# Paired product layout, router weights on GpSimd, reordered last chunk and tail in an attention and mixture-of-experts kernel

## The chip, the cores and the metric

One core of a Trainium2 chip runs the whole program. The metric is the device time of one execution in microseconds (us), lower is better. TensorE is called PE, VectorE DVE, ScalarE ACT, GpSimd POOL and SyncE SP. SP issues the plain transfers, POOL issues the gathers and scatters.

## The reference

The model is one gated convolution over a context of shape (8, 256, 512) and one feed-forward layer with 16 experts and a shared expert, both added to `x`. Cut to what matters:

```python
# attention-like mixer: 32 heads of 8 channels, sequence length 512
kv  = einsum('bhil,bhjl->bijhl', k, v)            # k = v = ctx: 36 distinct pairs of channels
y   = causal_convolution(kv, ssm_kernel) + kv * D # one Toeplitz matrix of taps per head
out = einsum('bijhl,bhil->bjhl', y, q)            # q = layernorm(x): 64 products, summed by eights
x   = x + out
# feed-forward
h      = layernorm(x)                             # 2048 tokens of 512
scores = softmax(h @ gate_w.T)                    # 16 experts, top 4, weights normalised
slots  = first 256 tokens of each expert, in order
y      = sum over experts of w * ((silu(xg @ w_gate) * (xg @ w_up)) @ w_down)   # inner width 352
shared = (silu(h @ sw_gate) * (h @ sw_up)) @ sw_down                            # inner width 704
x      = x + y + shared
```

## The kernel before

Every engine has its own program, written out by hand, and semaphores order them. Nothing is planned by a scheduler: what stands first in an engine's program runs first, and a wait holds everything behind it on that engine.

**Precision.** Each fp32 operand of a large product is split in a high part (rounded by ACT) and a low part (the rest, subtracted by POOL or DVE), and three products high*high, high*low, low*high are added (`PASSES`). So each piece of weights or data passes ACT and then DVE or POOL before PE may use it.

**Mixer.** There are 8 groups (`NG`) of 4 heads (`GH`). For head `n`, POOL makes the 36 channel pairs `kv` (`pairs`), ACT and POOL split them, PE multiplies with the Toeplitz blocks into the PSUM tile `yb` (`convolve`, 30 matmuls), DVE multiplies `yb` with the queries into `prod` (`multiply`, 15 instructions on 2048 elements, by halves of 30 instructions for the first four heads) and sums eights of them into `oT` (`add_up`). PE waits with head `n + 1` for the products of head `n` (`d_mul`), since `yb` holds one head.

**Shared expert.** Group `g - 1` is normalised, transposed and passed through `gate_up` (six parts, 24 matmuls each) while group `g` is convolved, and `down(g - 2)` makes its output: two tiles of 17 matmuls each, of which the first two are for the 64 inner columns that are left over from 704 (`REST`). The second of these two has 64 rows, all others have 128.

**Router.** DVE turns the logits into scores, finds the top 4, and computes the weights (`weights`), ranks and slots in two rounds: round 0 for the first 12 tiles of tokens, round 1 for the last 4. `rt_c` and `rt_mm` are the hand-over to three small matmuls and back. `one_hot(e)`, `slots(e)` and `decode(e)` give the token numbers `slot_rows` of expert `e`.

**Experts.** `gather(e)` on POOL fetches 256 rows into `xg`, PE transposes them (`rows_t`), ACT and DVE split them (`round_rows`, `low_rows`), PE runs three `expert_gu` and one `expert_down`, ACT weighs the result (`weigh`) and POOL adds it to the output (`scatter`). SP loads the raw weights `raw_w[k]` (1.4 MB) and `raw_d[k]` of the next experts into two slots, ACT and DVE split them into `ew` and `ed` (`split_w` and `low_w`, four parts each). From expert 1 on, a unit holds: two `expert_gu`, `slots(e + 2)`, `rows_t(e + 1)`, `expert_down(e - 1)`, the third `expert_gu`.

In this order PE leaves the mixer: `mixed_out(7)`, `down(6)`, `normalised(7)`, `gate_up(7, 0)`, router, `gate_up` 1 and 2, the three small matmuls, `gate_up` 3 to 5, `slots(0)`, `down(7)` tile 0, `slots(1)`, tile 1, `rows_t(0)`, `expert_gu(0, 0)`.

## Time and profile before

| | before |
|---|---|
| median of 3 runs | 664.18 us (661.24 to 664.54) |
| the profiled execution, its own time | 665.34 us |
| its span, first to last instruction | 663.5 us |
| PE busy | 609.0 us, 92% of the span |
| DVE busy | 506.9 us, 76% |
| POOL busy | 344.7 us, 52% |
| ACT busy | 283.6 us, 43% |
| mean granted TensorE clock | 0.973 of full speed |

The profiled execution's own time is 1.8 us above its span, and 1.2 us above the median of the runs. Busy times are sums over a program with three stages (mixer with shared expert to about 370 us, router and last chunk to about 440 us, experts after that), so they say only that PE is the fullest engine. What an edit is worth is read from the stage in which it lies.

### The profile page before, as it was taken

The page shows a single profiled execution, that of the slowest core. Times are in us where ns is not written, and L with a number is a line of the kernel's source. Part 1 is how long each engine was busy: PE and PEld are TensorE (multiplying, and loading weights), DVE is VectorE, ACT ScalarE, POOL GpSimd, SP SyncE. Part 2 cuts the span into 40 slices and gives each one's busy share as a digit, 9 for nine tenths or more (in the row PEclk, how much of TensorE's full clock was granted, in tenths as well). Part 3 has the DMA queues.
Part 4 walks back from the last instruction along what each step waited for, and adds up shares of the span by engine and source line. Part 5 has one row for each costly group of instructions (what it writes and reads, how often), then busy time and mean ns, then how long its engine had stood idle before and what let it go on. Part 6 is the DMA issues. An engine that isn't in the chain of part 4 may idle for free.

```text
span 663.5 us, 13617 instructions
## 1 busy us (share of the span) xinstructions
PE 609.0 (92%) x4487; PEld 568.0 (86%) x4487; DVE 506.9 (76%) x1248; ACT 283.6 (43%) x503; POOL 344.7 (52%) x467
## 2 busy tenths in 40 slices
PE   2867999999999999999999779889999999999982
PEld 2866997999989989989999578789999999999981
DVE  5897978959778778588698958698887878878630
ACT  3433542433423424234241233356656656656530
POOL 5796787856666676668551124216334443334321
PEclk9978999999999999999999989899999999999997
DMA  6664603424225124041130144567888878888442
GB/s 156 201 154 156 191 33 97 126 64 134 59 64 158 63 79 142 32 124 34 63 96 1 48 146 143 172 183 220 250 245 240 226 200 239 240 239 234 95 62 32
DMA packets 50386, 90.31 MB, mean 136 GB/s; under 512 B 3920, under 2 KB 20304, under 8 KB 50336
## 3 DMA queue, kind: packets, MB, share of 16 engines
q1 hardware_dynamic: 43168, 72.89, 35.7%
q0 software_dynamic: 7168, 16.78, 12.1%
q8 instruction: 28, 0.46, 0.3%
q14 instruction: 22, 0.18, 0.1%
HBM read 72.71 MB, written 16.94 MB: 135 GB/s over the span
## 4 chain that ended last, share of the span: by engine, by line
PE 74%; DVE 9%; issue 8%; POOL 4%; DMA 2%; ACT 1%; DVEq 0%; SPq 0%; POOLq 0%; ACTq 0%
PE gu L524 15%; PE yb L461 15%; PE gu L653 13%; PE mb L668 9%; PE gu L549 8%; PE yb L653 6%; PE mb L441 3%; DVE prod L1171 2%; PE yb L441 2%; DVE prod L1174 2%; POOL midl L1009 1%; PE gu L542 1%; DMA sw_raw<-in_L_ffn_sw_up_dram 1%; PE yb L627 1%; DVE oT L1190 1%
## 5 line engine op out<-in xcount | busy, mean ns | idle before, releaser
L461 PE MATMUL yb<-kvh,toep 128*128 128x288 f32 x640 | 140.6, 306 | 10.1 <-DVE prod L1174 8.8
L524 PE MATMUL gu<-xT,sw 128*128 128x256 f32 (+2 forms) x1152 | 144.4, 284 | 3.8 <-issue 3.8
L524 PEld LDWEIGHTS gu<-xT,sw 128*128 128x128 f32 (+2 forms) x1152 | 140.3, 184 | 4.3 <-issue 4.0
L1171 DVE TENSOR_TENSOR prod<-yb,qT 128x96 f32<-128x96 f32 (+11 forms) x288 | 112.5, 418 | 40.3 <-PE yb L461 39.2
L461 PEld LDWEIGHTS yb<-kvh,toep 128*128 128x128 f32 x640 | 109.8, 197 | 12.1 <-issue 9.2
L1001 POOL TENSOR_TENSOR kvl<-kv,kvh 128x1152 fp32r<-128x1152 f32 x31 | 83.4, 2691 | 59.7 <-ACT kvh L750 59.5
L993 POOL TENSOR_TENSOR kv<-kT 128x256 f32 (+3 forms) x248 | 113.3, 498 | 0.0
L461 PE MATMUL yb<-kvl,toep 128*128 128x288 f32 x320 | 97.4, 304 | 0.0
L1174 DVE TENSOR_TENSOR prod<-yb,qT 128x96 f32<-128x96 f32 (+10 forms) x252 | 93.4, 389 | 0.0
L750 ACT ACTIVATE kvh<-kv 128x1152 fp32r<-128x1152 f32 x32 | 37.4, 1168 | 91.4 <-POOL kv L993 48.5
L1190 DVE TENSOR_REDUCE oT<-prod 128x256 f32<-128x2048 f32 x32 | 72.7, 2272 | 0.1
L668 PE MATMUL mb<-ed,midh 128*128 128x512 f32 (+1 forms) x192 | 62.5, 407 | 1.9 <-ACT midh L897 1.9
L1009 POOL TENSOR_TENSOR midl<-mid,midh 128x256 fp32r<-128x256 f32 x40 | 33.1, 835 | 58.7 <-ACT midh L766 48.7
L461 PEld LDWEIGHTS yb<-kvl,toep 128*128 128x128 f32 x320 | 63.1, 197 | 0.0
L1448 DVE TENSOR_TENSOR ew<-raw_w,ew 128x704 fp32r<-128x704 f32 x64 | 55.5, 890 | 0.3 <-ACT ew L862 0.3
L549 PE MATMUL gu<-sd,midh 128*128 128x512 f32 x160 | 51.3, 402 | 0.4 <-POOL midl L1009 0.4
L653 PE MATMUL gu<-xT,ew 128*128 128x256 f32 x384 | 48.4, 287 | 1.8 <-DVE xT L1456 1.8
L653 PEld LDWEIGHTS gu<-xT,ew 128*128 128x128 f32 x384 | 47.6, 195 | 2.0 <-issue 2.0
L1075 POOL MEMSET carrier<- 128x1 f32 x16 | 1.6, 99 | 89.5 <-DVE slot_rows L1442 89.5
L653 PE MATMUL gu<-xgT,ew 128*128 128x256 f32 x384 | 47.2, 282 | 0.6 <-DVE ew L1448 0.6
L653 PEld LDWEIGHTS gu<-xgT,ew 128*128 128x128 f32 x384 | 46.4, 190 | 0.8 <-issue 0.8
L862 ACT ACTIVATE ew<-raw_w 128x704 fp32r<-128x704 f32 x64 | 45.4, 778 | 3.1 <-DMA raw_w<-in_L_ffn_w_up_dram 3.1
(168 smaller groups left out, 1009.5 us busy)
## 6 DMA issues: line engine op xcount, KB each, us to landing
toep<-toeplitz_taps SPq DMA_DIRECT2D x32, 512.0 KB, 3.7
raw_w<-in_L_ffn_w_gate_dram SPq DMA_DIRECT2D x16, 704.0 KB
raw_w<-in_L_ffn_w_up_dram SPq DMA_DIRECT2D x16, 704.0 KB
raw_d<-in_L_ffn_w_down_dram SPq DMA_DIRECT2D x16, 512.0 KB, 4.3
c_t<-in_ctx_dram SPq DMA_DIRECT2D x16, 256.0 KB, 4.7
x_t<-in_x_dram SPq DMA_DIRECT2D x16, 256.0 KB, 4.8
normalised_tokens<-xn SPq DMA_DIRECT2D x16, 256.0 KB, 2.9
out_dram<-yo SPq DMA_DIRECT2D x16, 256.0 KB, 2.9
```

The costliest lines, as they stand in the source:

```text
L461: last = pe.matmul(yb[:, lb, 0:PW], toep[s][:, a, d:d + P], rhs[:, s, m, :], start=(i == 0), stop=(i == len(steps) - 1))
L524: last = pe.matmul(gu[0:m, i % 2, u * GT:(u + 1) * GT], sw[:, c, a, col:col + m], xT[:, c, b, :], start=(c == 0 and (a, b) == PASSES[0]), ...
L549: last = pe.matmul(gu[:, t, :], (midh, midl)[a][:, j, cols], sd[:, j, b, :], start=False, stop=(j == SJ - 2 and (a, b) == PASSES[-1]))
L653: last = pe.matmul(egu[j][0:m, u * CAP:(u + 1) * CAP], ew[k][:, c, a, col:col + m], xgT[k][:, c, b, :], start=(c == 0 and (a, b) == PASSES ...
L668: last = pe.matmul(mb[:, h, :], lhs[0:EK[j], EJ * k + j, h * P:(h + 1) * P], ed[k][0:EK[j], j, b, :], start=(j == 0 and (a, b) == PASSES[0 ...
L862: act.activation(ew[k][:, c, 0, :], raw_w[k][:, c, :], ACT.Copy).then_inc(ew_h, 1)
L993: last = pool.tensor_tensor(kv[:, s, :, POFF[d]:POFF[d] + w], src[:, :, 0:w], src[:, :, d * B:HD * B], ALU.mult)
L1001: pool.tensor_tensor(kvl[:, s, :, :], kv[:, s, :, :], kvh[:, s, :, :].bitcast(fp32), ALU.subtract)\
L1171: last = dve.tensor_tensor(prod[:, s, lo:hi, d * B:HD * B, d], yb[:, lo:hi, POFF[d]:POFF[d] + w], q[:, lo:hi, 0:w], ALU.mult)
L1174: last = dve.tensor_tensor(prod[:, s, lo:hi, 0:w, HD - d], yb[:, lo:hi, POFF[d]:POFF[d] + w], q[:, lo:hi, d * B:HD * B], ALU.mult)
L1190: dve.tensor_reduce(oT[:, :, hl * HD * B:(hl + 1) * HD * B], prod[:, s, :, :, :], AX.X, ALU.add)\
L1448: dve.tensor_tensor(ew[k][:, c, 1, :], raw_w[k][:, c, :], ew[k][:, c, 0, :].bitcast(fp32), ALU.subtract).then_inc(ew_l, 1)
```

## The change

Six parts. (1) `prod` holds pairs of neighbouring columns next to each other, so that two products are written side by side and the next pair lies 64 bytes further; before, each product lay alone, 32 bytes from the next. (2) The second matmul of a tile in `down` has 128 rows: the low part of `sd` is made for both halves. (3) The last tile of `down(6)` is cut in two, with the transposes of `normalised(7)` in between, and so is the last tile of `down(7)`, with `rows_t(0)` in between; `slots(0)` goes ahead of `gate_up(7, 5)`; DVE takes the last two low parts of the chunk (`low_mid`, `last_l`). (4) `weights` moves from DVE to POOL, and the columns that don't depend on scores are written earlier (`slot_columns`). (5) SP issues the loads of the second expert's raw weights only when the rows of the first have landed, and ACT and DVE split them inside the first expert's unit. (6) The last expert's `down` runs over parts outside and halves inside, and takes a part when it is ready; the wait for all additions to the output moves from POOL to SP.

```diff
-        prod = place("prod", [P, 2, LB, HD * B, HD], fp32)
+        prod = place("prod", [P, 2, LB, HD * B // 2, HD, 2], fp32)
...
             sp.wait_ge(gu_mm, SJ * NG)
+            sp.wait_ge(rows_in[0], 16 * HALVES)
             load_raw_w(1, 1)
             load_raw_d(1, 1)
...
             sp.wait_ge(xn_out, 16 * TT * NG)
+            sp.wait_ge(added, 16 * HALVES * E)
...
-                    pe.matmul(gu[:, t, :], midh[0:REST, SJ - 1, cols], sd[0:REST, SJ - 1, 1, :],
-                              start=False, stop=False)
-                    for j in range(SJ - 1):
+                    if -1 in chunks:
...
+                        pe.matmul(gu[:, t, :], midh[0:2 * REST, SJ - 1, cols], sd[0:2 * REST, SJ - 1, 1, :],
+                                  start=False, stop=False)
+                    for j in chunks:
...
-            down(NG - 2)
+            down(NG - 2, [0])
+            down(NG - 2, [1], range(-1, 2))
             normalised(NG - 1)
+            down(NG - 2, [1], range(2, SJ - 1))
             gate_up(NG - 1, 0)
...
-            for i in range(3, SJ):
-                gate_up(NG - 1, i)
+            gate_up(NG - 1, 3)
+            gate_up(NG - 1, 4)
...
+            def last_down(e, k):
+                pe.wait_ge(ed_h, e + 1)
+                pe.wait_ge(ed_l, e + 1)
+                for j in range(EJ):
+                    pe.wait_ge(e_midh, EJ * e + j + 1)
+                    pe.wait_ge(e_midl, EJ * e + j + 1)
+                    for h in range(HALVES):
...
+                        if j == EJ - 1:
+                            last.then_inc(e_dn, 1)
...
             slots(0)
+            gate_up(NG - 1, 5)
             down(NG - 1, [0])
             slots(1)
-            down(NG - 1, [1])
+            down(NG - 1, [1], range(-1, 2))
             rows_t(0, 0)
+            down(NG - 1, [1], range(2, SJ - 1))
...
-                if not (isinstance(e, int) and e == 0):
-                    for c in range(LB):
-                        split_w(e + 1, 1 - k, c)
+                for c in range(LB):
+                    split_w(e + 1, 1 - k, c)
                 e_silu(e, k, 0)
...
-            for c in range(LB):
-                split_w(1, 1, c)
...
+            def weights(i):
...
+                pool.wait_ge(rt_go, i + 1)
+                step(pool.tensor_tensor(w, scp[:, tiles, 0:E],
+                                        r_rec[:, tiles].unsqueeze(2).broadcast_to([P, width(tiles), E]), ALU.mult))
+                step(pool.tensor_copy(part(3), w))
+                step(pool.tensor_tensor(left, w, part(3), ALU.subtract))
+                step(pool.tensor_copy(part(4), left))
+                step(pool.tensor_tensor(w, left, part(4), ALU.subtract))
+                pool.tensor_copy(part(5), w).then_inc(rt_w, 1)
...
+            weights(1)
+            for i in range(1, SJ - 2):
                 low_mid(NG - 1, i)
...
-            pool.wait_ge(added, 16 * HALVES * E)
...
+                        last = dve.tensor_tensor(prod[:, s, lo:hi, d * B // 2:HD * B // 2, d, :], pair, first, ALU.mult)
                         if d:
...
+                            last = dve.tensor_tensor(prod[:, s, lo:hi, 0:w // 2, HD - d, :], pair, second, ALU.mult)
...
-                                  prod[:, s, :, :, :], AX.X, ALU.add)\
+                                  prod[:, s, :, :, :, :].rearrange("p c a i u -> p c a u i"), AX.X, ALU.add)\
...
-            weights(0)
             low_tokens(NG - 1)
...
-            weights(1)
             places()
+            dve.wait_ge(rt_w, 2)
             values(0, 2)
+            one_hot(0)
             middle(NG - 1, 3)
-            one_hot(0)
+            decode(0, 0)
             middle(NG - 1, 4)
-            decode(0, 0)
+            low_mid(NG - 1, 4)
             middle(NG - 1, 5)
             one_hot(1)
+            low_mid(NG - 1, 5)
...
-            low_w(1, 1, 0)
-            low_w(1, 1, 1)
             low_rows(0, 0)
```

On PE, behind `down(6)` (mb<-ident,xn are the transposes of `normalised(7)`; gu<-xT,sw 80x256 is the start of `gate_up(7, 0)`), the end of the second tile of `down(6)` reads like this before:

```order
L549 MATMUL gu<-sd,midh 128x512 x2
L549 MATMUL gu<-sd,midl 128x512
L549 MATMUL gu<-sd,midh 128x512 x2
L549 MATMUL gu<-sd,midl 128x512
L441 MATMUL mb<-ident,xn 128x128 x8
L524 MATMUL gu<-xT,sw 80x256 x12
```

and in the changed kernel like this:

```order
L565 MATMUL gu<-sd,midh 128x512 x2
L565 MATMUL gu<-sd,midl 128x512
L452 MATMUL mb<-ident,xn 128x128 x8
L565 MATMUL gu<-sd,midh 128x512 x2
L565 MATMUL gu<-sd,midl 128x512
L565 MATMUL gu<-sd,midh 128x512 x2
L565 MATMUL gu<-sd,midl 128x512
L565 MATMUL gu<-sd,midh 128x512 x2
L565 MATMUL gu<-sd,midl 128x512
L535 MATMUL gu<-xT,sw 80x256 x12
```

Nine matmuls of the tile now stand behind the transposes, between them and `gate_up(7, 0)`.

On POOL, between the end of the mixer and the first gather (L972 and L974 make the normalisation of group 7, L1067 clears the gather buffers, L1009 is `low_mid`), the program before is:

```order
L974 TENSOR_TENSOR tnb<-tnm,trs 128x2
L1067 MEMSET xg_126 128x1024
L1067 MEMSET xg_127 128x1024
L1009 TENSOR_TENSOR midl<-mid,midh 128x256 x5
L1075 MEMSET carrier 128x1
```

and in the changed kernel (L1111 to L1117 are `weights`, 128x12x16 in round 0 and 128x4x16 in round 1):

```order
L1009 TENSOR_TENSOR tnb<-tnm,trs 128x2
L1111 TENSOR_TENSOR wt<-scp,r_rec 128x12x16
L1125 MEMSET xg_127 128x1024
L1125 MEMSET xg_128 128x1024
L1111 TENSOR_TENSOR wt<-scp,r_rec 128x4x16
L1113 CAST V<-wt 128x4x16
L1114 TENSOR_TENSOR wrest<-wt,V 128x4x16
L1115 CAST V<-wrest 128x4x16
L1116 TENSOR_TENSOR wt<-wrest,V 128x4x16
L1117 CAST V<-wt 128x4x16
L1044 TENSOR_TENSOR midl<-mid,midh 128x256 x3
L1133 MEMSET carrier 128x1
```

Twelve instructions of the router are new here, and the gather waits for three low parts of the chunk where it waited for five.

On ACT, at the start of the experts (xT<-yb is `round_rows(0)`, the gathered rows of expert 0; ew_138 and ew_139 hold the split weights of expert 1), before:

```order
L862 ACTIVATE ew_122<-raw_w_124 128x704 x2
L862 ACTIVATE ew_138<-raw_w_136 128x704 x4
L884 ACTIVATE xT<-yb 128x4x128 x2
L891 ACTIVATE sil<-gu 128x256
```

and in the changed kernel:

```order
L900 ACTIVATE ew_123<-raw_w_125 128x704 x2
L922 ACTIVATE xT<-yb 128x4x128 x2
L900 ACTIVATE ew_139<-raw_w_137 128x704 x4
L929 ACTIVATE sil<-gu 128x256
```

The four roundings of expert 1's weights moved behind the rows of expert 0 and still stand ahead of its first activation.

## Rows read from the trace of the kernel before

**Rows 1.** Busy time by stretch: PE, PEld, DVE, ACT, POOL, clock, DMA.

```profile
100.00:200.00 100.00, 99.22 (x702) 91.90 (x701) 78.67 (x208) 34.51 (x59) 69.57 (x104) 1.00 0.32 92
```

**Rows 2.** Who PE waited for: us in total, times, longest us.

```profile
PE yb L461 <- DVE prod L1174: 8.8, 7, 3.2
```

**Rows 3.** Timeline of PE, one tile of a down: start us, us, instruction.

```profile
150.92 0.39 PE L540 MATMUL gu<-sd,midh 128*128 128x512 f32 x1
...
152.91 0.39 PE L549 MATMUL gu<-sd,midl 128*128 128x512 f32 x1
...
153.59 0.39 PE L549 MATMUL gu<-sd,midl 128*128 128x512 f32 x1
...
155.18 1.03 PE L441 MATMUL mb<-ident,xn 128*128 128x128 f32 x8
```

**Rows 4.** Timeline of DVE in the mixer; brackets hold idle before.

```profile
157.89 1.26 DVE L1209 TENSOR_TENSOR xT<-mb,xT 128x512 fp32r<-128x512 f32 x2
160.34 1.10 DVE L1171 TENSOR_TENSOR prod<-yb,qT 128x256 f32<-128x256 f32 x2 [1.20 <-PE yb L461]
...
164.48 0.39 DVE L1219 TENSOR_TENSOR mid<-sil,gu 64x256 f32<-64x256 f32 x1
164.81 2.25 DVE L1190 TENSOR_REDUCE oT<-prod 128x256 f32<-128x2048 f32 x1
```

**Rows 5.** Timeline of DVE and PE at the end of the mixer.

```profile
360.74 1.10 DVE L1171 TENSOR_TENSOR prod<-yb,qT 128x256 f32<-128x256 f32 x2 [1.98 <-PE yb L461]
...
367.48 1.09 PE L441 MATMUL mb<-ident,oT 128*128 128x128 f32 x8 [1.15 <-DVE oT L1190]
```

**Rows 6.** Timeline from the second tile of down(6) to gate_up(7, 0).

```profile
372.56 1.52 ACT L720 ACTIVATE xn<-x,tnb,trs 128x512 f32<-128x512 f32 x2 [4.36 <-POOL tnb L974]
...
377.73 1.03 PE L441 MATMUL mb<-ident,xn 128*128 128x128 f32 x8
...
382.57 4.49 PE L524 MATMUL gu<-xT,sw 128*80 128x256 f32 x24 [3.81 <-issue]
```

**Rows 7.** Timeline of PE behind the router's chain on DVE.

```profile
395.92 0.28 PE L615 MATMUL yb<-chosen_b,before_in_b 128*128 128x256 bf16 x1 [1.85 <-DVE tot_b L1310]
```

**Rows 8.** Timeline from the last chunk to the first expert.

```profile
403.04 2.27 POOL L1009 TENSOR_TENSOR midl<-mid,midh 128x256 fp32r<-128x256 f32 x1 [5.58 <-ACT midh L766]
...
405.57 0.74 POOL L1009 TENSOR_TENSOR midl<-mid,midh 128x256 fp32r<-128x256 f32 x1 [0.26 <-ACT midh L766]
...
406.28 0.56 PE L627 MATMUL yb<-VH,onehot 128*128 128x12 bf16 x16
...
411.02 1.67 POOL L1077 DMA_INDIRECT xg<-normalised_tokens,slot_rows  x1 [0.19 <-POOL carrier L1075]
...
417.56 1.09 PE L441 MATMUL yb<-ident,xg 128*128 128x128 f32 x8 [0.88 <-DMA xg<-normalised_tokens,slot_rows]
...
420.49 7.27 PE L653 MATMUL gu<-xT,ew 128*128 128x256 f32 x48 [1.84 <-DVE xT L1456]
```

**Rows 9.** Timeline, the second expert's weights and the first two units.

```profile
406.47 0.37 SPq L401 DMA_DIRECT2D raw_w<-in_L_ffn_w_gate_dram  x1
...
412.96 2.84 ACT L862 ACTIVATE ew<-raw_w 128x704 fp32r<-128x704 f32 x4 [3.14 <-DMA raw_w<-in_L_ffn_w_up_dram]
...
432.46 5.95 PE L653 MATMUL gu<-xgT,ew 128*128 128x256 f32 x48 [0.55 <-DVE ew L1448]
...
439.67 0.56 PE L627 MATMUL yb<-VH,onehot 128*128 128x12 bf16 x16 [1.27 <-DVE onehot L1425]
```

**Rows 10.** Timeline of the last down and the last addition.

```profile
645.12 1.03 PE L668 MATMUL mb<-ed,midh 128*128 128x512 f32 x2 [1.87 <-ACT midh L897]
...
652.59 1.55 POOL L1090 DMA_INDIRECT out_dram<-xn,slot_rows  x1 [0.40 <-issue]
```

**Rows 11.** Two stretches of two us: us, PE busy, clock, DMA share, GB/s.

```profile
420.00:422.00 2.00, 1.51 (x7) 0.51 0.31 111
...
658.00:660.00 2.00, 0.00 (x0) 0.50 0.00 0
```

More of the change, by code:

```diff
@@ L181, in xattn_moe_kernel @@
         wtmp = place("wtmp", [P, TE], fp32)
+        wrest = place("wrest", [P, TE], fp32)
         V = place("V", [P, TE, 6], bf16)
@@ L285, in xattn_moe_kernel, with by_tile, width @@
         ROUND = [slice(0, TT * (NG - 2)), slice(TT * (NG - 2), NT)]
+        def by_tile(t, tiles):
+            return t[:].rearrange("p (e n) -> p n e", n=NT)[:, tiles, :]
+        def width(tiles):
+            return tiles.stop - tiles.start
         block = es.enter_context(nc.Block())
@@ L527, in gate_up, with down @@
                 last.then_inc(gu_mm, 1)
-            def down(g, tiles=range(TT)):
+            def down(g, tiles=range(TT), chunks=range(-1, SJ - 1)):
                 last_chunk = isinstance(g, int) and g == NG - 1
@@ L671, in expert_down @@
                     last.then_inc(e_dn, 1)
+            def last_down(e, k):
[5 more added lines that the diff above has]
+                    for h in range(HALVES):
+                        if j == 0:
+                            pe.wait_ge(e_ok, HALVES * e - HALVES + h + 1)
+                        for a, b in PASSES:
+                            lhs = (midh, midl)[a]
+                            last = pe.matmul(mb[:, h, :], lhs[0:EK[j], EJ * k + j, h * P:(h + 1) * P],
+                                             ed[k][0:EK[j], j, b, :], start=(j == 0 and (a, b) == PASSES[0]),
+                                             stop=(j == EJ - 1 and (a, b) == PASSES[-1]))
+                        if j == EJ - 1:
+                            last.then_inc(e_dn, 1)
             def unit(e, k, before, next2):
@@ L1061, in _, with step @@
             inverse_t(NG - 1)
+            parts = [0]
+            def weights(i):
+                tiles = ROUND[i]
+                w, left = by_tile(wt, tiles), by_tile(wrest, tiles)
+                part = lambda c: V[:, :, c:c + 1].rearrange("p (e n) a -> p n (e a)", n=NT)[:, tiles, :]
+                def step(ins):
+                    parts[0] += 1
+                    ins.then_inc(rt_step, 1)
+                    pool.wait_ge(rt_step, parts[0])
+                pool.wait_ge(rt_go, i + 1)
[6 more added lines that the diff above has]
+                pool.tensor_copy(part(5), w).then_inc(rt_w, 1)
+            weights(0)
             pool.wait_ge(conv, H)
@@ L1098, in unit @@
                     scatter(e - 1, 1 - k)
-            for i in range(1, SJ):
+            weights(1)
+            for i in range(1, SJ - 2):
                 low_mid(NG - 1, i)
@@ L1232, in chunk_sum @@
                     dve.tensor_tensor(yo[:, t, :], gu[:, t, :], x1_tile(g, t), ALU.add).then_inc(dn_ok, 1)
-            def by_tile(t, tiles):
-                return t[:].rearrange("p (e n) -> p n e", n=NT)[:, tiles, :]
-            def width(tiles):
-                return tiles.stop - tiles.start
             def scores(i):
@@ L1482, in unit @@
             def unit(e, k, before, next2):
-                late = not (isinstance(e, int) and e == 0)
                 if before:
```

70 lines of the change are left out of this document (36 added, 34 removed).

## The prediction

> **What bounds the kernel now.** I read the busy times by stretch first. From 100 to 200 us PE is busy 99.2 of 100 us while DVE has 78.7 [rows 1], and the stretches to 370 us and from 440 to 640 us look the same: there only work that leaves PE can shorten anything. Next I read who PE waited for, and the idle time in brackets in the timeline. Nearly all idle time lies in three places: the first 90 us, where PE waits 8.8 us for the products of DVE, 1.1 us of it once more at the end of the mixer [rows 2, 5]; the passage from the mixer to the experts, with gaps of 3.81, 1.85, 0.88, 1.84, 0.55 and 1.27 us [rows 6 to 9]; and the end, with a gap of 1.87 us and more than 9 us from the last issue of an addition to the end of the span [rows 10, 11]. Gaps cost twice here: behind the gap of 1.84 us 48 matmuls take 7.27 us, and the same 48 take 5.95 us behind a gap of 0.55 us [rows 8, 9]; the granted clock from 420 to 422 us is 0.51 [rows 11], the level of 1.2 instead of 2.4 GHz. So a long gap is followed by slow work, worth about 1.4 us each time.
>
> **Part 1, the products.** A head writes 2048 products. From 160.34 to 164.48 us they take 4.14 us [rows 4], 2.0 ns each. In the same stretch two instructions of 512 elements on packed data take 1.26 us [rows 4], at most 1.2 ns an element. Both read PSUM; what differs is the write, which steps 32 bytes per product. The new layout writes two together. No row shows such a write, so the cost lies between the two: nothing gained (4.14 us) and the packed rate (2048 x 1.2 = 2.5 us, plus the start of 15 instructions, about 0.05 us each: 3.2 us). I take 3.2 us, since the sum of eights already reads 2048 elements at 1.1 ns in 2.25 us [rows 4] and nothing else in the write is unusual: 0.9 us a head. The heads done by halves have half as many elements in each instruction, and the start of an instruction weighs more there, so I take 0.1 us a half. This counts only where PE waits for products. In the first 90 us the chain runs through DVE: seven halves give 0.6 us, and then one full head shortens the wait of 3.2 us [rows 2]; but behind that, PE waits for the shared weights, which follow DVE's earlier work alone. The gap of about 1.1 us at the seventh head goes. Together 1.6 us (bounds 0 and 2.6). In 100 to 360 us DVE has 21% of slack [rows 1] and a gain is hidden behind PE. At the end of the mixer DVE starts the last products at 360.74 us and PE waits 1.15 us for the sum [rows 5]: 0.9 us (bounds 0 and 1.1). Sum: **-2.5 us**.
>
> The Trainium skill, SBUF — State Buffer, in its note on 16-byte lines, says that full bandwidth needs at least two hits in a line; by it the old write has one hit a line and the new one has two, and the sum of eights, which now reads every 8 bytes, keeps two. The rows of the old write agree with a cost of nearly twice; the new write is shown by no row. By that rule alone the products would take 3.2 us as well.
>
> **Part 2, 128 rows in the second matmul of a tile.** A tile takes 155.18 - 150.92 = 4.26 us, while three of its ordinary matmuls take 153.59 - 152.91 = 0.68 us, 0.227 each [rows 3]. Seventeen at that pitch are 3.87 us. So the change to 64 rows and back costs 0.39 us. It is exposed, since PE is the bound. Fourteen tiles (groups 0 to 6) lie on PE's path: 14 x 0.39 = **-5.5 us** (bounds: 14 x 0.2, if only the way in or out is saved, and 14 x 0.5). The extra low part on DVE is in one instruction at the start, with twice the partitions and the same length.
>
> **Part 3, the passage to gate_up(7, 0).** Now PE ends the tile, transposes at 377.73 us, and then stands idle 3.81 us, because DVE does round 0 of the weights ahead of `low_tokens`; after that 24 matmuls take 4.49 us at the low clock [rows 6], where half of 5.95 us is 2.9 at most [rows 9]. In the change the transposes stand eight matmuls into the second tile, 1.8 us, so at about 375.3 us on the old clock; `xn` is complete at 374.08 [rows 6] and doesn't hold them. Behind them PE has nine matmuls, 2.05 us. In this time ACT needs 0.6 us for each half and DVE 0.6 us behind it (1.26 for two [rows 4]), about 1.8 us in all, and DVE is free since the weights are gone. Cover and chain are equal within 0.3 us: the gap of 3.8 us goes, and the clock's 1.6 us with it: **-5.4 us** (bounds -3.5, if the clock still falls or a rest of the gap stays, and -5.7).
>
> The router's chain to the three small matmuls keeps its length; PE still waits about 1.85 us [rows 7]. POOL's six instructions of round 1 run beside it. A low part on POOL takes 0.74 us alone and 2.27 us beside the one-hot instruction of DVE [rows 8], so the two engines hold each other up: **+0.2 us** (bounds 0 and +1.5, five DVE instructions that each wait for one short one on POOL).
>
> **Part 4, half chunk, gather, second expert's weights.** Count from the small matmuls at 395.92 us. Before, expert 0 starts at 420.49, 24.6 us later [rows 7, 8]. PE's own work there is now 72 matmuls (8.8 us, plus 1.4 for the clock behind the gap), two `slots` (0.5 each in flight [rows 8]), 34 matmuls of `down` (34 x 0.227 = 7.7), eight transposes 0.9, small matmuls 0.3: 20.1 us. Two waits could stand in it. `down(7)` needs the low part of part 5, which DVE makes behind the second one-hot (2.3 us): about 0.5 us of stall. And the gathered rows: `slots(0)` comes one part (2.9 us) earlier, and POOL no longer has two low parts, one of them slow, ahead of the gather, so it is issued at about +9.4 us instead of +15.1. It took 6.5 us from issue to the transposes beside the load of raw weights [rows 8]; at the same price it is there at +15.9, ahead of the transposes at +17.8. So expert 0 starts at +20.7: 3.9 us earlier, at the high clock, 1.4 more.
>
> Part of this goes back. The raw weights of expert 1 were issued at 406.47 and there at 412.96 us, 6.5 us later [rows 9]. Now SP issues them when the rows land, about +15, so they land at +21.5. Then ACT rounds four parts, 2.84 us [rows 9], ahead of the first activation of expert 0: +24.4. Behind it DVE has, in this order, two of the low parts, the first product, the third low part, decode, the second product, the rows of expert 1, the fourth low part: about 7.5 us, so expert 1 can start at about +32.0. PE has finished expert 0 at +30.8 and idles 1.2 us. Before it was 432.46 - 395.92 = +36.5 [rows 9]. DVE then has the same rest as before up to the third one-hot, for which PE already waits 1.27 us [rows 9]; PE idles about 1.8 us there, and the net gain at that place is **-4.2 us** (bounds: -0.5, if the load takes 10 us because rows, stores and the next weights share it, and -5.5). Behind it, PE is busy all the time for fourteen units, and the lead neither grows nor shrinks.
>
> **Part 5, the tail.** Before, PE waits 1.87 us until the third part is split, and its 18 matmuls begin at the low clock [rows 10]. Now the first twelve, 2.7 us, lie over that wait, so PE ends 1.87 + 1.6 us earlier or more. The additions are then bound by POOL: 1.55 us an issue and 0.3 to 0.4 between [rows 10]. The second issue starts about 2.5 us earlier: **-2.5 us** (bounds -1.5 and -3.9).
>
> **Part 6, the last wait.** The last issue ends at 654.14 us; at 658 us nothing moves any more [rows 10, 11], yet the span ends at 663.5. So about 5.5 us of closing work on POOL follow its wait for the additions. With the wait on SP it can begin at the end of the last issue and lie beside the transfer: **-3.7 us**. No row shows it running alone; the bounds are -3.8 and 0, if closing POOL itself waits for its transfers.
>
> **Sum.** -2.5 - 5.5 - 5.4 + 0.2 - 4.2 - 2.5 - 3.7 = -23.6 us. Against its own 665.34 us this gives 641.7; the three runs have a median of 664.18, which gives 640.6. I predict **641.0 us**.
>
> **Rivals.** (a) Closing POOL waits for its transfers, wherever the semaphore is waited for. For it: the 5.5 us begin only when the transfer is over; against it: nothing orders them once the wait is gone. Time: 644.7. (b) The late load of expert 1 takes the place of the gather as what ends last: from 406 to 413 us it had the queue almost alone, now it shares it with the second gather and two stores. If it lands 3.5 us later than I think, PE idles nearly 5 us ahead of expert 1, and the clock falls too: 645.5. (c) POOL and DVE exclude each other more than I think in the router's chain: at its upper bound, 642.5. The Trainium skill, SBUF — State Buffer, on the port pair of VectorE and GpSimd, calls it an exclusive lock held for a whole instruction; the 2.27 us against 0.74 us in the rows agree. (d) Slower than before: the paired write or the sum over a stride of 8 bytes costs more, and DVE becomes the bound of the mixer. A head has about 10.2 us of PE, of which DVE is busy 79%, so 2.1 us are free; to lose all of the gain over 28 heads it takes another 0.85 us a head, that is products and sum 3.0 us longer than now, 9.4 instead of 6.4. At 4 us longer the time is about 670 us. For it speaks only that no row shows either pattern.
>
> **How the numbers follow.** Chances: my forecast 0.58, (a) 0.19, (b) 0.12, (c) 0.06, (d) 0.03, anything else 0.02. A measurement of this kernel tells 0.5%, 3.3 us, from no change. All cases but (d) and the rest are faster by more than that: faster 0.96, same 0.02, slower 0.02. For the range: the lower end adds what the bounds still hold on the good side (1.0 for the tiles, 1.4 if the clock doesn't fall at the router either, 1.3 in part 4, 1.0 in the tail, not all at once): 636. The upper end takes in (a) and (b), and the case that the products give nothing on PE's path (+2.5) with a smaller slip: 647.
>
> **What would show it.** In the changed kernel: 15 products of a head within 3.2 us and a sum that still takes 2.3; a tile of `down` at 3.9 us; no gap of PE over 0.5 us ahead of `gate_up(7, 0)`; the wait for the router's chain as before; the first gather issued within 10 us of the small matmuls; ACT waiting for raw weights ahead of expert 0's first activation, and gaps of one to two us of PE ahead of expert 1 and the third one-hot; the last down without a gap, and the last issue of an addition about 6 us ahead of the end. The prediction is wrong above all if the mixer changes its pace by more than the tiles, or if the gaps after the gather are 5 us long.

## The result, and the profile after

| | before | after |
|---|---|---|
| median | 664.36 us (661.24 to 665.25, 4 runs) | **642.45 us** (640.7 to 643.2, 4 runs) |
| the profiled execution, its own time | 665.34 us | 642.93 us |
| its span | 663.5 us | 641.1 us |
| PE / DVE / POOL busy | 609.0 / 506.9 / 344.7 us | 594.9 / 479.0 / 350.5 us |
| mean granted TensorE clock | 0.973 | 0.983 |

The ratio of after to before is 0.9673 (95% interval 0.9651 to 0.9695), 21.7 us. The prediction was 641.0 us.

First the timeline of the changed kernel, piece by piece in order of time (start us, us, instruction; in brackets the idle time before it and what ended it). The pieces answer to [rows 3 to 10].

```profile
149.02 0.39 PE L554 MATMUL gu<-sd,midh 128*128 128x512 f32 x1
...
152.88 1.03 PE L452 MATMUL mb<-ident,xn 128*128 128x128 f32 x8
...
345.36 0.66 DVE L1320 TENSOR_SCALAR V<-reset,row_f 128x256 bf16<-128x256 f32 x1
345.71 0.74 DVE L1321 TENSOR_SCALAR V<-tok_i,row_f 128x256 bf16<-128x256 int32 x1
...
355.29 0.72 DVE L1233 TENSOR_TENSOR prod<-yb,qT 128x256 f32<-128x256 f32 x2 [1.89 <-PE yb L472]
...
358.31 0.18 DVE L1235 TENSOR_TENSOR prod<-yb,qT 128x32 f32<-128x32 f32 x1
...
358.86 2.28 DVE L1249 TENSOR_REDUCE oT<-prod 128x256 f32<-128x2048 f32 x1
...
361.19 1.09 PE L452 MATMUL mb<-ident,oT 128*128 128x128 f32 x8 [0.30 <-DVE oT L1249]
...
363.12 0.47 PE L554 MATMUL gu<-sd,midh 128*128 128x512 f32 x1 [0.84 <-ACT midh L804]
...
368.91 1.03 PE L452 MATMUL mb<-ident,xn 128*128 128x128 f32 x8
...
371.84 2.97 PE L535 MATMUL gu<-xT,sw 128*80 128x256 f32 x24
...
383.69 0.28 PE L634 MATMUL yb<-chosen_b,before_in_b 128*128 128x256 bf16 x1 [1.87 <-DVE tot_b L1360]
...
394.62 2.92 POOL L1135 DMA_INDIRECT xg<-normalised_tokens,slot_rows  x1 [0.31 <-issue]
...
400.15 0.37 SPq L410 DMA_DIRECT2D raw_w<-in_L_ffn_w_gate_dram  x1
400.25 1.03 PE L452 MATMUL yb<-ident,xg 128*128 128x128 f32 x8
...
402.28 1.00 POOL L1135 DMA_INDIRECT xg<-normalised_tokens,slot_rows  x1 [0.64 <-issue]
...
403.18 5.88 PE L672 MATMUL gu<-xT,ew 128*128 128x256 f32 x48
...
406.62 2.83 ACT L900 ACTIVATE ew<-raw_w 128x704 fp32r<-128x704 f32 x4 [4.58 <-DMA raw_w<-in_L_ffn_w_up_dram]
...
411.42 1.09 PE L452 MATMUL yb<-ident,xg 128*128 128x128 f32 x8 [1.96 <-DMA xg<-normalised_tokens,slot_rows]
...
415.47 5.94 PE L672 MATMUL gu<-xgT,ew 128*128 128x256 f32 x48
...
422.68 0.56 PE L646 MATMUL yb<-VH,onehot 128*128 128x12 bf16 x16 [1.26 <-DVE onehot L1475]
...
626.10 0.63 PE L703 MATMUL mb<-ed,midh 128*128 128x512 f32 x2
...
633.19 1.55 POOL L1148 DMA_INDIRECT out_dram<-xn,slot_rows  x1 [0.30 <-issue]
```

What to see: a tile of `down` takes 152.88 - 149.02 = 3.86 us (4.26 in [rows 3]). The products of a head run from 355.29 to 358.49, 3.2 us, and the sum of eights still takes 2.28. The gap of 3.81 us of [rows 6] is gone, and the 24 matmuls behind it take 2.97 us. There is a new gap of 0.84 us ahead of `down(6)`. The router's wait is as it was (1.87 us; 1.85 in [rows 7]). Raw weights are issued at 400.15 us, the moment at which the first rows have landed, and PE takes those rows at 400.25 without waiting. Then it waits 1.96 us for the rows of the **second** expert and 1.26 us at what all texts here call the third one-hot (it is `one_hot(3)`, that of the fourth expert, and the fourth in PE's order).

The following sum goes through the span by places that both traces have (PE instructions, apart from the last two lines). It gives all 22.4 us between the spans:

| part | predicted | in the trace |
|---|---|---|
| first 110 us (products) | -1.6 | -0.7 |
| 14 tiles with 128 rows | -5.5 | -5.5 |
| end of the mixer (products) | -0.9 | -0.9 |
| passage to `gate_up(7, 0)` and router, with the gap ahead of `down(6)` | -5.2 | -5.2 |
| small matmuls to the third one-hot | -4.2 | -4.8 |
| tail, to the last issue | -2.5 | -2.4 |
| last issue to the end of the span | -3.7 | -3.0 |
| sum | -23.6 | -22.4 |

### The profile page after: what moved, and what is told of

It is laid out like the page before. It is cut to its first block, busy times and chain, and to the rows that moved or that the text cites. A ratio compares the mean times of both kernels' runs of the same rounds, so it can differ in the third digit from the quotient of the medians.

```text
span 641.1 us, 13621 instructions
## 1 busy us (share of the span) xinstructions
PE 594.9 (93%) x4487; PEld 562.4 (88%) x4487; DVE 479.0 (75%) x1234; ACT 283.1 (44%) x503; POOL 350.5 (55%) x477
## 4 chain that ended last, share of the span: by engine, by line
PE 78%; DVE 7%; POOL 5%; issue 4%; DMA 3%; ACT 2%; SPq 0%; POOLq 0%; DVEq 0%; ACTq 0%
PE gu L535 16%; PE yb L472 15%; PE gu L672 12%; PE mb L687 10%; PE gu L565 7%; PE yb L672 7%; PE mb L452 4%; PE yb L452 2%; POOL kvl L1036 2%; POOL kv L1028 2%; DMA xg<-normalised_tokens,slot_rows 1%; DMA toep<-toeplitz_taps 1%; PE yb L646 1%; ACT kvh L788 1%; DVE oT L1249 1%
## 5 line engine op out<-in xcount | busy, mean ns | idle before, releaser
L472 PE MATMUL yb<-kvh,toep 128*128 128x288 f32 x640 | 138.9, 304 | 8.5 <-DVE prod L1235 3.4
L535 PE MATMUL gu<-xT,sw 128*128 128x256 f32 (+2 forms) x1152 | 142.3, 282 | 0.0
L535 PEld LDWEIGHTS gu<-xT,sw 128*128 128x128 f32 (+2 forms) x1152 | 138.2, 181 | 0.3
L472 PEld LDWEIGHTS yb<-kvh,toep 128*128 128x128 f32 x640 | 108.4, 195 | 9.9 <-issue 8.5
L1233 DVE TENSOR_TENSOR prod<-yb,qT 128x96 f32<-128x96 f32 (+11 forms) x288 | 78.7, 284 | 42.4 <-PE yb L472 41.3
L1235 DVE TENSOR_TENSOR prod<-yb,qT 128x96 f32<-128x96 f32 (+10 forms) x252 | 67.6, 268 | 0.0
L687 PE MATMUL mb<-ed,midh 128*128 128x512 f32 x180 | 57.5, 400 | 0.0
L1044 POOL TENSOR_TENSOR midl<-mid,midh 128x256 fp32r<-128x256 f32 x38 | 28.3, 753 | 40.8 <-ACT midh L804 40.8
L565 PE MATMUL gu<-sd,midh 128*128 128x512 f32 x160 | 49.8, 392 | 0.3 <-DVE midl L1291 0.3
L672 PE MATMUL gu<-xT,ew 128*128 128x256 f32 x384 | 47.0, 282 | 0.0
```

The costliest lines, as they stand in the source:

```text
L472: last = pe.matmul(yb[:, lb, 0:PW], toep[s][:, a, d:d + P], rhs[:, s, m, :], start=(i == 0), stop=(i == len(steps) - 1))
L535: last = pe.matmul(gu[0:m, i % 2, u * GT:(u + 1) * GT], sw[:, c, a, col:col + m], xT[:, c, b, :], start=(c == 0 and (a, b) == PASSES[0]), ...
L565: last = pe.matmul(gu[:, t, :], (midh, midl)[a][:, j, cols], sd[:, j, b, :], start=False, stop=(j == SJ - 2 and (a, b) == PASSES[-1]))
L672: last = pe.matmul(egu[j][0:m, u * CAP:(u + 1) * CAP], ew[k][:, c, a, col:col + m], xgT[k][:, c, b, :], start=(c == 0 and (a, b) == PASSES ...
L687: last = pe.matmul(mb[:, h, :], lhs[0:EK[j], EJ * k + j, h * P:(h + 1) * P], ed[k][0:EK[j], j, b, :], start=(j == 0 and (a, b) == PASSES[0 ...
L1233: last = dve.tensor_tensor(prod[:, s, lo:hi, d * B // 2:HD * B // 2, d, :], pair, first, ALU.mult)
```

## The experiments

Each kernel is the changed one with the edit named. In this table "timed" is the distance to the changed kernel: its ratio to before less the changed kernel's (0.9670, the mean of 0.9673 and, beside the last four kernels, 0.9668), times 664 us; each has some 2 us of uncertainty. "Trace" is one profile against the profile of the changed kernel: from `normalised(1)` on PE, near 108 us, to the last issue of an addition, which leaves out the start of the program.

| kernel | median, us | ratio to before (95%) | timed | trace |
|---|---|---|---|---|
| a1, 64 rows again | 647.6 | 0.9759 (0.9732 to 0.9786) | +5.9 | +4.5 |
| a2, old products | 646.5 | 0.9733 (0.9709 to 0.9757) | +4.2 | +3.8 |
| a3, last wait on POOL | 644.6 | 0.9705 (0.9678 to 0.9732) | +2.3 | -0.2 (span +2.6) |
| a4, old last `down` | 643.4 | 0.9698 (0.9671 to 0.9726) | +1.9 | +2.0 |
| a5, weights not held | 647.4 | 0.9753 (0.9725 to 0.9781) | +5.5 | +5.1 |
| a6, weights of the router on DVE | 645.9 | 0.9740 (0.9708 to 0.9771) | +4.6 | +3.4 |
| a7, `down(6)` whole | 643.5 | 0.9709 (0.9675 to 0.9743) | +2.6 | +1.5 |
| a8, old order on PE | 647.4 | 0.9758 (0.9727 to 0.9788) | +5.8 | +5.8 |
| c0, the changed kernel again | 642.2 | 0.9668 (0.9648 to 0.9687) | | +0.1 |
| w5, a second wait | 643.1 | 0.9673 (0.9657 to 0.9690) | +0.2 | -0.2 |
| w3, four moves | 639.4 | 0.9627 (0.9611 to 0.9643) | -2.9 | -3.2 |
| w6, both | 640.2 | 0.9638 (0.9610 to 0.9667) | -2.1 | -1.6 |

### One part undone: a1 to a4

```diff
-  pe.matmul(gu[:, t, :], midh[0:2 * REST, SJ - 1, cols], sd[0:2 * REST, SJ - 1, 1, :], ...
+  pe.matmul(gu[:, t, :], midh[0:REST, SJ - 1, cols], sd[0:REST, SJ - 1, 1, :], ...
```

> The changed kernel, with the second matmul of each tile of down back at 64 rows (the low half of the left-over part of sd is left out of the product, as in the kernel before). Theory: the switch to 64 rows and back costs 0.39 us a tile and is exposed, so all 16 tiles get 4.2 to 4.3 us long instead of 3.87 to 3.98, the expert stage keeps its pace, and the time is 642.4 + 14 x 0.39 = 647.9 us, up to 648.7 if the two tiles of the last chunk count too. Rival: the tiles got shorter for another reason (the new order or the product layout), then the time stays within 1 us of 642.4 and a tile stays under 4.0 us.

The timeline of PE in this kernel:

```profile
144.97 0.48 PE L554 MATMUL gu<-sd,midh 128*128 128x512 f32 x1
145.37 0.50 PE L556 MATMUL gu<-sd,midh 64*128 64x512 f32 x1
145.80 0.73 PE L565 MATMUL gu<-sd,midh 128*128 128x512 f32 x2
```

From the start of the first matmul to the second it is 0.40 us and from there to the third 0.43, where neighbours of 128 rows follow each other at 0.23. So both ways cost, 0.2 us each. From 108 us to `gate_up(7, 0)` the trace loses 4.7 us over 12 tiles, 0.39 a tile. The theory holds. Up to the first rows it is 5.1 us, and 0.7 of it comes back at the second gather, for which PE then waits less.

a2 restores `prod` and the sum as they were:

```diff
-  prod = place("prod", [P, 2, LB, HD * B // 2, HD, 2], fp32)
+  prod = place("prod", [P, 2, LB, HD * B, HD], fp32)
```

> The changed kernel, with the old layout of prod and its old sum. Theory from the trace of the changed kernel: the write costs 1.1 us a head on DVE, but PE sees only about 0.7 us of it in the first 90 us and 0.85 us at the end of the mixer, so a head's products take 4.1 us again and the time is 643.5 to 644.5 us. Rival, the sizes of the prediction: 1.6 + 0.9 us, 644.9 us or more, with the wait of PE for products back at 8.8 us in total. Second rival: DVE has so little slack that the mixer's pace changes too, more than 646 us.

The timeline of its PE at the end of the mixer:

```profile
352.32 0.37 PE L472 MATMUL yb<-kvh,toep 128*128 128x288 f32 x1 [1.04 <-DVE prod L1233]
...
363.31 1.09 PE L452 MATMUL mb<-ident,oT 128*128 128x128 f32 x8 [1.14 <-DVE oT L1249]
364.94 0.47 PE L554 MATMUL gu<-sd,midh 128*128 128x512 f32 x1 [0.53 <-issue]
...
370.50 0.39 PE L554 MATMUL gu<-sd,midh 128*128 128x512 f32 x1
```

My theory fell: I had put +0.85 us at the end of the mixer, and it is +3.7 between group 6 and `gate_up(7, 0)`. There is a second wait at 352.32 us that the kernel before does not have. By the trace it comes from `slot_columns`, which the change put on DVE between two heads of the last group (345.36 to 347.31 in the changed kernel); no run moves these columns alone. The faster products pay for these 2 us; without them PE waits three times, and the first tile of `down(6)` takes 370.50 - 364.94 = 5.6 us instead of 4.0: the granted clock is 0.57 from 365 to 369 us. So about 1.6 of the 3.7 us are the clock behind the waits. The second rival (the whole mixer slows) is out: from group 2 to group 6 the distances agree within 0.3 us.

a3 moves `wait_ge(added, ...)` from the end of SP to the end of POOL.

> The changed kernel, with the wait for all additions to the output back at the end of POOL's program. Theory: closing work of POOL of about 5.3 us can start at the end of the last issue only if POOL waits for nothing; with the wait it starts when the last addition has landed. From the last issue's end to the span's end it then takes 9.4 us instead of 6.4, and the time is 645.4 us. Rival: the closing work ends with the transfer in any case and the 3 us came from the tail's other part (the last down); then the time stays within 0.7 us of 642.4.

Its last issue is

```profile
632.85 1.55 POOL L1147 DMA_INDIRECT out_dram<-xn,slot_rows  x1 [0.30 <-issue]
```

It ends at 634.40 us, the span at 643.6: 9.2 us, where the changed kernel has 641.1 - 634.74 = 6.4. That is 2.8 us where 3.0 was expected, and 2.3 us in the timed runs.

a4 puts `expert_down` back in `last_unit`.

> The changed kernel, with the last expert's down by halves outside and parts inside, so that its first matmul waits for all three parts. Theory: PE waits about 1.9 us ahead of it and the 18 matmuls start at the low clock; the issue of the last addition comes 2.4 us later, 644.8 us. Rival: the additions are bound by POOL alone, one after the other from the first, and the order inside the last down gives less than 1 us: 643.4 us or less.

Its PE timeline has the gap of [rows 10] again:

```profile
625.68 0.70 PE L687 MATMUL mb<-ed,midh 128*128 128x512 f32 x2 [1.87 <-ACT midh L935]
```

From the third one-hot to the last issue it is 2.4 us longer, as in the theory; the timed runs show 1.9 and can't tell it from the rival's 1.

### The weights held back: a5 and w5

```diff
   sp.wait_ge(gu_mm, SJ * NG)
-  sp.wait_ge(rows_in[0], 16 * HALVES)
   load_raw_w(1, 1)
```

> The changed kernel, in which SP issues the raw weights of expert 1 as soon as gate_up(7, 5) is done, without the wait for the rows of expert 0. Nothing else moves: ACT and DVE still split them inside expert 0's unit. Theory: the wait keeps 2 MB out of the queue while the first rows are fetched; without it they are issued at about 393.7 us, at the same time as the first gather, whose rows come 1 to 3 us later than 400.1; PE, which reaches the transposes at 400.25, waits as long, and expert 0 starts at 404 to 406 instead of 403.2. On the other side the weights are there when ACT is free at 402, so ACT no longer waits 4.6 us for them, and the second gather has the queue alone and PE no longer waits 2.0 us for it. Net at expert 1: between -1.5 and +1.5 us, time 641 to 644 us. Rival A: the wait is worth what the gather took at its worst before, the rows come more than 3 us later, and the time is over 645 us. Rival B: the wait only costs, the rows come at the same time and the time is 640.4 us or less.

Here are the same stretches in this kernel by windows (us, busy time of PE, PEld, DVE, ACT, POOL, clock, DMA share, GB/s), and then its timeline:

```profile
394.00:396.00 2.00, 1.73 (x8) 1.06 (x7) 2.00 (x4) 0.53 (x1) 1.79 (x1) 1.00 1.09 391
396.00:398.00 2.00, 2.00 (x24) 1.62 (x23) 2.00 (x4) 0.00 (x0) 0.00 (x0) 1.00 1.02 379
...
402.00:404.00 2.00, 1.79 (x9) 1.79 (x10) 0.00 (x0) 0.58 (x1) 0.83 (x1) 0.50 0.71 169
```

```profile
392.87 2.93 POOL L1134 DMA_INDIRECT xg<-normalised_tokens,slot_rows  x1 [0.31 <-issue]
...
402.21 1.97 PE L451 MATMUL yb<-ident,xg 128*128 128x128 f32 x8 [3.53 <-DMA xg<-normalised_tokens,slot_rows]
...
407.81 6.01 PE L671 MATMUL gu<-xT,ew 128*128 128x256 f32 x48
```

and the windows of the changed kernel:

```profile
394.00:396.00 2.00, 2.00 (x11) 1.65 (x10) 1.97 (x2) 1.51 (x3) 1.69 (x2) 1.00 0.45 119
396.00:398.00 2.00, 1.70 (x10) 0.95 (x9) 2.00 (x4) 0.27 (x1) 1.54 (x1) 1.00 0.04 16
```

Rival A came true. In the changed kernel the queue is all but empty (share 0.04) in the stretch in which the second issue of the gather ends, and its rows are there 2.6 us after that (400.15 less 397.54). Without the wait they share a full queue with 2 MB of weights and need 6.4 us (402.21 less 395.80). PE waits 3.53 us, and the clock is at 0.50 in the next stretch: the transposes take 1.97 us instead of 1.03 and the nine matmuls that stand behind them come at half the pace. Counted from the small matmuls, the transposes start 3.7 us later and expert 0 starts 6.4 us later, so 2.7 us are slow work behind the wait; the 1.3 us that come back before expert 1 don't cover it. So holding the load is worth 5 us here. I had expected a draw, because I put the rows 1 to 3 us later and not 3.7, and because I left out the clock behind the wait.

w5 adds a second wait of the same kind:

```diff
   load_raw_w(1, 1)
+  sp.wait_ge(rows_in[1], 16 * HALVES)
   load_raw_d(1, 1)
```

> The changed kernel with a second wait of the same kind: SP loads the second expert's raw gate/up weights when the rows of the first have landed, and its raw down weights, the stores and the next loads only when the rows of the second have landed as well. Theory: in the changed kernel the second gather is issued at 402.3 us into a full queue (share 1.0 or more to 412) and lands at 411.3, 1.96 us after PE wants it. With the wait it lands by 408, PE does not wait, and expert 1 starts when its weights are split: 1 us earlier, 641.4 us against 642.4 (start of the program at the same place), and the third one-hot comes 1 us earlier too. Rival: the raw gate/up weights alone fill the queue, the second gather still comes at 410 or later, and nothing is gained: 642.4 us.

PE no longer waits for the second rows (from expert 0's start to expert 1's start it is 11.0 us instead of 12.3; what it waits for now is the split of expert 1's weights, 0.96 us), but this profile lost as much 20 us earlier, at the router:

```profile
383.60:385.60 2.00, 2.00 (x12) 1.98 (x13) 1.66 (x4) 1.10 (x2) 1.94 (x4) 0.66 0.00 0
```

and the same window of the changed kernel, counted from the small matmuls:

```profile
383.69:385.69 2.00, 2.00 (x18) 1.98 (x19) 1.66 (x4) 1.10 (x2) 1.94 (x4) 1.00 0.04 8
```

Behind equal gaps of 1.86 and 1.87 us the clock falls in one execution and not in the other (48 matmuls in 7.43 and 5.88 us). The timed runs show no gain (+0.2 us, with some 2 us of uncertainty). So whether the second wait helps by itself stays open within 2 us.

### The passage: a6, a7, a8

a6 makes both rounds of `weights` on DVE, ahead of `low_tokens` and ahead of `places`. a7 and a8 change PE's order alone:

```diff
 a7
-            down(NG - 2, [1], range(-1, 2))
+            down(NG - 2, [1])
             normalised(NG - 1)
-            down(NG - 2, [1], range(2, SJ - 1))
 a8
-            slots(0)
             gate_up(NG - 1, 5)
+            slots(0)
             down(NG - 1, [0])
             slots(1)
-            down(NG - 1, [1], range(-1, 2))
+            down(NG - 1, [1])
             rows_t(0, 0)
-            down(NG - 1, [1], range(2, SJ - 1))
```

> The changed kernel, with the router's weights on DVE (both rounds, at the places of the kernel before; the columns that depend on no score stay where they are now, and the two copies between the steps stay away). Theory: round 0 holds low_tokens by about 4.3 us of DVE, of which the nine matmuls of the cut tile cover 2, so PE idles 2 to 2.6 us ahead of gate_up(7, 0) and its 24 matmuls take 4.4 us at the low clock; round 1, some 2.5 to 3 us of DVE, lies on the chain to the first one_hot, so PE waits about 3 us there and the first gather goes out 2.5 to 3 us later. Together +6 to +8.5 us: 648.4 to 651 us. Rival: the weights beside POOL already cost DVE as much by the lock of the two engines as they save in round 1, then only the passage counts: +4, 646.4 us.

> The changed kernel, with the second tile of down(6) whole and the transposes of normalised(7) behind it; the weights stay on POOL. Theory: the chain behind the transposes (ACT 0.6, DVE 0.6 for each half, 1.8 in all) lies bare, PE idles 1.5 us ahead of gate_up(7, 0), and whether the clock falls behind such a gap is open: 643.9 us without, 645.4 us with it. Rival: the split does nothing, since the weights on DVE made all of the old gap: 642.4 us.

> The changed kernel, with PE's order of the kernel before in the last chunk: gate_up(7, 5) ahead of slots(0), and down(7) tile 1 whole ahead of rows_t(0). Theory: DVE's decode and with it the last parts of the chunk wait for slots(0) 3 us longer, the gather is issued 3 us later and its rows land at 403; the transposes and the splitting of the rows lie bare behind them. Expert 0 starts 3 to 4.8 us later: 645.4 to 647.2 us. Rival: since the second expert's weights and rows follow the same issue, the delay grows further behind it, over 648 us; or it is taken back there, under 644 us.

The waits of PE in a6 from 370 to 400 us (in total, times, longest):

```profile
PE yb L634 <- DVE tot_b L1349: 1.9, 1, 1.9
PE yb L646 <- DVE onehot L1465: 1.7, 1, 1.7
PE gu L535 <- issue: 1.6, 1, 1.6
```

In a6 the gap ahead of `gate_up(7, 0)` is 1.57 us and not 2 to 2.6, and the clock doesn't fall behind it (24 matmuls in 3.01 us). The chain to the one-hot is 1.4 us longer, not 2.5 to 3: round 1 takes 2.3 us of DVE, but the ranks behind it are 0.6 us faster without POOL beside them (two `tensor_scalar` instructions take 0.50 and 0.71 us beside POOL and 0.29 each alone), and 0.3 us of waiting for PE's small matmuls go. Behind the wait of 1.66 us for the one-hot the clock does fall (24 matmuls in 4.60 us). Up to expert 0 all this costs 4.7 us, and 1.3 come back, since PE waits less for the second gather. My +6 to +8.5 was too high, and the 4.6 us timed are near the rival's 4: the lock does take part of what round 1 saves.

a7 costs 1.5 us in the trace, as expected without a fall of the clock: PE idles 1.62 us ahead of `gate_up(7, 0)`, and the 24 matmuls behind it take 3.01 us. That gap speaks against the rival. The timed runs (642.2 to 645.9 us) can't tell a7 from the changed kernel. So of the old gap and its slow matmuls (3.81 + 1.5 us), the move of the weights alone removes about 3.7 us, and the cut tile the last 1.6; with the weights on DVE the cut tile leaves 1.57, so the two cover each other in part. a8 costs 5.8 us in both views, above my 3 to 4.8: DVE waits 3.65 us for the slots, PE then 2.33 us for the last low part ahead of `down(7)`, and 1.83 us for the split rows behind bare transposes.

```profile
394.34 0.58 PE L554 MATMUL gu<-sd,midh 128*128 128x512 f32 x1 [2.33 <-DVE midl L1290]
```

I had costed no wait ahead of `down(7)`. The granted clock falls to 0.5 behind each of the two waits of PE, for 3.4 us (from 394.5 and from 408.2 us).

### What is left: w3, w6 and c0

The four moves of w3, in short:

```text
DVE:  low_w(0,0,0..1), +decode(1,1)+, low_w(0,0,2..3), chunk_sum(7,0)      (decode stood behind chunk_sum)
DVE, unit of expert 0:  e_middle(0) low_w(0) low_w(1) e_low(0) e_middle(1) low_w(2) decode low_w(3) low_rows e_low(1)
ACT, unit of expert 0:  e_silu(0) split_w(0) split_w(1) e_round(0) split_w(2) e_silu(1) split_w(3) e_round(1)
DVE:  values(4, E) behind expert 1's unit                                   (was: behind expert 0's)
PE:   down(6) waits for its last part at its last part only                 (was: at its start)
```

w6 is w3 with the second wait of w5 added, and c0 is the changed kernel once more.

> The changed kernel with four moves: the second decode stands between the low parts of expert 0's weights on DVE (second gather issued 1.8 us earlier); in expert 0's unit ACT and DVE take the first activations and products ahead of the second expert's weights; the slot values of experts 4 to 15 (2.6 us of DVE) come one unit later, behind the third one-hot; and down(6) starts without waiting for its last part. Theory: the wait of 1.96 us for the second rows, the one of 1.26 us at the third one-hot and the one of 0.84 us ahead of down(6) go, less 0.3 us for what is late next: 3.7 us, 638.7 us (start at the same place). Rival 1: the second gather meets the same full queue and lands no earlier, then expert 1 gains nothing and only 2.1 us are left, 640.3 us. Rival 2: the moved values make the same wait one unit later, 640 us.

> The four moves of the kernel before this one, with the second wait of SP added. Theory: both together do not add up, since each takes the same wait of 1.96 us away: 638.2 to 638.7 us, expert 1 bound by DVE (its weights and rows are split at about 413.5 us). Rival: the gather is what holds expert 1 in the version without the second wait, then this one is 1.5 us or more faster than it.

> The changed kernel itself once more, beside the three that follow, to see how far its runs and its first 100 us scatter. In the eight profiles so far, PE reaches the first tile of down at 96.3 to 99.0 us; where the Toeplitz taps of the second head come late it is 98 or 99, else about 97. Expected: a median of 641 to 643.5 us, and one of these two starts; everything behind xn of group 1 at the same distances as before, to 0.1 us.

w3 takes 639.35 us, 2.9 us less than the changed kernel, and the interval of its ratio does not touch that of c0. Up to the transposes of `normalised(7)` it is 1.1 us ahead (the gap of 0.84 us is gone), the second gather goes out 2.2 us earlier as counted from the first rows, and PE waits neither for it nor at the third one-hot. Its one wait over 0.4 us between the first rows and the place where the third one-hot was waited for is

```profile
413.26 5.93 PE L676 MATMUL gu<-xgT,ew 128*128 128x256 f32 x48 [0.47 <-DVE xgT L1520]
```

By these waits neither rival came true; the timed 2.9 us alone lie between the 3.7 expected and the rivals' 2.1 to 2.4. Its profile also met the fallen clock at the router, 1.1 us; without it the trace would give 4.3 us, above the 3.7 expected.

The profile of w6 shows what the second wait can cost once DVE has no spare: everything that SP issues later moves too, and the third expert's weights come late. Its timeline:

```profile
419.86 2.84 ACT L905 ACTIVATE ew<-raw_w 128x704 fp32r<-128x704 f32 x4 [3.56 <-DMA raw_w<-in_L_ffn_w_up_dram]
...
435.97 0.56 PE L651 MATMUL yb<-VH,onehot 128*128 128x12 bf16 x16 [1.28 <-DVE onehot L1490]
```

With `values` now in expert 1's unit, DVE can't make the delay up, and the wait for a one-hot is back one unit later. The lead shrinks by 2.4 us there, where I expected no loss. This is one execution, of 642.43 us; the six timed runs lie between 638.51 and 644.42 us, and they don't show w6 to be slower than w3.

c0 repeats the changed kernel: 642.19 us, and behind `normalised(1)` every distance within 0.2 us of the first profile's, apart from a wait of 0.88 instead of 1.96 us for the second rows that expert 1's weights take back.

## Why the prediction was right

**Part 1, products (-2.5; -1.6 in the trace).** The duration was right, 3.2 us a head, and so was the sum of eights. What PE got of it in the first 90 us can't be read from one pair of traces. PE reaches `normalised(1)` at 109.96 us before. In the twelve profiles with the new layout it is 105.9 to 106.7 us in five and 108.0 to 109.5 in seven, where the shorter tiles alone give 0.8. These are PE's waits from 40 to 110 us in the changed kernel and in a4, which have the same instructions there:

```profile
PE yb L472 <- DVE prod L1235: 2.5, 1, 2.5
...
PE yb L472 <- DMA toep<-toeplitz_taps: 1.8, 1, 1.8
```

```profile
PE yb L472 <- POOL kvl L1036: 3.0, 1, 3.0
```

In the late cluster DVE's products end the longest wait of a convolution in this stretch (2.5 us), in the early one POOL's low part of `kv` (3.0 to 4.3 us). So the step that failed is "several halves and one full head shorten PE's wait": in part POOL takes over as the releaser. The clock adds to the scatter. The windows of the changed kernel (us, busy time of PE, clock, DMA share, GB/s) are

```profile
64.00:68.00 4.00, 2.49 (x15) 0.77 0.00 0
68.00:72.00 4.00, 4.00 (x29) 0.81 0.69 180
```

and in a4 the clock is 1.00 in both. All seven late profiles have a stretch at 0.5 that begins between 65.0 and 67.1 us, and none of the five early ones and not the kernel before has one there; from `normalised(0)` to `normalised(1)` it makes about 1 us of the 2. So the -0.7 us carry a fall of the clock that the kernel before was spared. What makes it fall in one execution and not in the other stays open. The -0.9 at the end of the mixer is right as a number by luck, as a2 shows: I costed `slot_columns` on DVE at nothing, and the layout covers it. The 0.84 us wait ahead of `down(6)` (its last part stands behind the sum on DVE, which PE now gets earlier) I had not seen either.

**Part 2, 128 rows (-5.5; -5.5).** Right, and a1 shows that both ways of the switch cost.

**Part 3, passage (-5.4 + 0.2; -5.2).** Right: no gap ahead of `gate_up(7, 0)`, high clock, the router's wait unchanged. Rival (c), the lock in the router's chain, is not seen in that wait. It is there behind it: two DVE steps beside POOL take 0.50 and 0.71 us, against 0.29 each in a6. The Trainium skill, SBUF — State Buffer, on the port pair, has this as a lock that the first to start keeps; the gather's second issue agrees, 2.92 us when DVE's one-hot started 0.25 us ahead of it, and 1.01 us in w5, where the one-hot started 0.17 us behind it.

**Part 4, half chunk, gather, late weights (-4.2; -4.8).** The sum was near, the chain was not. Expert 0 starts at +19.5 and not +20.7, because the clock did not fall at the router in this execution (1.4 us of my term; in w3 and w5 it did). Expert 1 starts at +31.8 against +32.0. But I had the late weights end last there, with PE idle 1.2 us ahead of expert 1. They were issued at +16.5 and not +15, because the gather's second issue took 2.92 us, and landed 6.5 us later as predicted; ACT does wait 4.58 us; PE's idle time is the 1.96 us for the second gather, issued into the queue that the same load fills. I had not costed that gather. Luck is in this term too. My working put the load of the weights at +15 where its own line has the rows at +15.9, so ACT is done with them at +25.8 and not at +24.4; but behind that expert 1 starts 6.0 us later and not 7.5, and the two slips cancel. Nor is the gather far ahead of the weights: in c0 PE waits only 0.88 us for the second rows, then 1.13 us for the split weights of expert 1, and expert 1 starts at +31.9 all the same. Rival (b) named the sharing and put 3.5 us on the wrong transfer.

**Part 5, tail (-2.5; -2.4).** Right; a4 gives it back.

**Part 6, last wait (-3.7; -3.0).** Mis-sized. The end comes 6.4 us after the last issue, not 5.7: the closing work of POOL does lie beside the last transfer, but not all of it, and what holds the remaining 0.7 us no row shows. Rival (a) is excluded by a3.

The edits undone one at a time add up to more (a1 to a8: 33 us timed, each with some 2 us of uncertainty) than the 22 us together. So the terms are not independent: a6 and a7 cover each other in part, and in a2 the products hide the slot columns.

## What to carry to other kernels

A load that nobody needs yet is best issued when the latency-bound transfer ahead of it has landed: holding 2 MB back for 6.5 us was worth 5 us. Without it the rows came 3.7 us later and PE's clock fell behind the wait, 2.7 us more, of which 1.3 us in all came back. But a wait on the issuing queue delays all that is behind it, so check the next gather and the next weights too: the second wait of the same kind gained nothing that the timed runs show. And when several edits are joined, cost each with the others in place: work moved onto an engine (the slot columns) may be free only because another edit made room there.

## What the runs showed of the hardware

- Two equal idle times of PE, 1.86 and 1.87 us at the same place of the same program, were followed by a granted clock of 0.66 and then 0.50 in one execution, and 1.00 in another, 1.1 us apart at the one-hot. The fall came in two of thirteen profiles of the changed kernel and its variants, and in that of the kernel before (1.85 us, 48 matmuls in 7.38 us). So behind gaps of this length the fall is not sure, and a comparison of two profiles has to look at it.
- A matmul of 64 rows between matmuls of 128 costs 0.2 us on the way in and 0.2 on the way out. The Trainium skill, TensorEngine Tiling (Array Packing), Key Properties, says that a change of tiling mode drains the engine; the two pitches of 0.40 and 0.43 us against 0.23 agree, for an operand that merely has fewer rows.
- The second indirect issue of the first gather on POOL took 2.91 to 2.94 us in the nine profiles in which a DVE instruction of 2.3 us had started 0.23 to 0.26 us ahead of it, 1.97 us in a8, where that had started 1.2 us ahead, and 1.01 us in the three in which the issue started first (a6, w5, w3).
